# A third bank for the exponents' scores, and the first feed-forward units as steps of the last attention group

## What is computed

```python
x = _layernorm(x + attn0(x))   # 16 heads of 16, causal, softmax(q k / 4) v, then w_out and b_out
x = _layernorm(x + ffn0(x))    # hidden 1024; wu, wg, wd are ternary: silu(x wu) * (x wg), then wd
x = _layernorm(x + attn1(x))   # 16 heads, 4 key/value heads; ALiBi bias; pairs inside a window of
                               # +-32 or with i < 64 or j < 64 are masked out; q from x * sigmoid(sum|x|)
x = _layernorm(x + ffn1(x))    # silu(x w_gate) * (x w_up), then w_down
```

## Time and profile before

| | us |
|---|---|
| median of 3 runs | 1046.7 |
| the profiled execution | 1047.7 |
| its span, first to last instruction | 1046.0 |
| TensorE, VectorE, ScalarE, GpSimd busy | 978.5, 696.0, 598.1, 348.4 |
| mean granted TensorE clock | 0.975 |
| layer 0: first exponent | 86.2 |
| layer 0: last group, and the barrier behind it | 299.6 to 338.3 |
| layer 1: first exponent | 511.3 |
| layer 1: last group, and the barrier behind it | 844.4 to 895.4 |

### The profile page before, as it was taken

The page is one execution under the profiler, slowest core; times in us unless marked ns, Lnnn a source line. Parts: engine busy times, 40 slices in busy tenths (PEclk is TensorE's granted clock), DMA queues, the critical chain, the costliest instruction groups (busy, mean ns, idle before and its releaser), DMA issues. The chain is left out here.

```text
span 1046.0 us, 18023 instructions
## 1 busy us (share of the span) xinstructions
PE 978.5 (94%) x6546; PEld 515.4 (49%) x6546; DVE 696.0 (67%) x1535; ACT 598.1 (57%) x1204; POOL 348.4 (33%) x418
## 2 busy tenths in 40 slices
PE   6798999999988999987899999999999999899997
PEld 4452333333334888663334343333434344698896
DVE  2877878888835666578887878788788824325423
ACT  4344777777775435344476777777676767322321
POOL 3031222221212445232336363433425243224323
PEclk9797999999999999999899999999999999999999
DMA  7552111212000200151615050322301000000001
GB/s 252 173 172 97 57 31 38 63 61 62 2 2 3 89 1 1 39 170 57 182 38 171 1 171 8 123 73 59 105 28 38 1 2 1 1 1 21 21 1 41
DMA packets 32996, 64.20 MB, mean 61 GB/s; under 512 B 6095, under 2 KB 22367, under 8 KB 30532
## 3 DMA queue, kind: packets, MB, share of 16 engines
q1 hardware_dynamic: 31564, 58.47, 18.1%
q0 software_dynamic: 1072, 3.80, 1.1%
q10 hardware_dynamic: 272, 0.79, 0.2%
HBM read 50.45 MB, written 12.32 MB: 60 GB/s over the span
## 5 line engine op out<-in xcount | busy, mean ns | idle before, releaser
L1102 ACT ACTIVATE prob<-ps 128x512 f32<-128x512 f32 (+6 forms) x896 | 434.6, 536 | 183.8 <-PE ps L1145 176.2
L1145 PE MATMUL ps<-qop,kop 98*128 98x512 bf16 (+14 forms) x1376 | 279.5, 290 | 4.7 <-ACT prob L1102 1.2
L1131 PE MATMUL ps<-kop,qop 96*128 96x512 bf16 (+3 forms) x896 | 232.3, 361 | 18.7 <-DVE maxes L1037 14.6
L1145 PEld LDWEIGHTS ps<-qop,kop 107*128 107x128 bf16 (+1 forms) x1376 | 105.6, 98 | 253.4 <-ACT prob L1102 211.0
L1174 PE MATMUL ps<-prob,vst 128*32 128x512 f32 (+4 forms) x1792 | 212.3, 545 | 6.2 <-POOL prob L974 3.3
L1037 DVE CUSTOM_DVE_ANT_0 sums<-ps,tri 128x128 bf16<-128x128 f32 (+7 forms) x256 | 181.5, 754 | 32.1 <-PE ps L1131 27.6
L974 POOL TENSOR_TENSOR prob<-prob,keep 128x384 int32<-128x384 int32 (+2 forms) x144 | 122.8, 854 | 205.6 <-ACT prob L1102 204.4
L1037 DVE CUSTOM_DVE_ANT_0 sums<-ps,table 128x960 bf16<-128x960 f32 x128 | 148.1, 1157 | 58.2 <-PE ps L1131 44.4
L1570 PE MATMUL ps<-xs,wffn 128*128 128x512 f32 x640 | 156.2, 398 | 3.7 <-PEq L805 2.2
L1037 DVE CUSTOM_DVE_ANT_0 tri<-ps,table 128x960 bf16<-128x960 f32 x128 | 147.6, 1153 | 4.3 <-PE ps L1131 4.3
L1468 POOL TENSOR_TENSOR hs<-hf,hs 128x512 fp32r<-128x512 f32 x64 | 83.0, 1298 | 158.1 <-ACT hs L1495 158.0
(11 more groups left out here) (103 smaller groups left out, 685.8 us busy)
## 6 DMA issues: line engine op xcount, KB each, us to landing
table<-in_table SPq DMA_DIRECT2D x32, 464.0 KB, 4.7
qop<-q_parts SPq DMA_DIRECT2D x96, 128.0 KB, 2.6
kop<-k_parts SPq DMA_DIRECT2D x48, 128.0 KB, 2.6
kop<-k_parts SPq DMA_DIRECT2D x48, 96.0 KB
q_parts<-qop SPq DMA_DIRECT2D x8, 384.0 KB, 3.8
q_parts<-kop SPq DMA_DIRECT2D x8, 384.0 KB, 2.6
x<-in_x SPq DMA_DIRECT2D x4, 512.0 KB, 5.8
k_parts<-qop SPq DMA_DIRECT2D x4, 384.0 KB, 2.7
```

The lines of the kernel that those rows point to most:

```text
L1102: nc.scalar.activation(prob[0:rows, q % 2, k % HG, lo % CH:lo % CH + hi - lo], ps[0:rows, t_bank(n, k), lo % CH:lo % CH + hi - lo], ACT.Ex ...
L1131: last = nc.tensor.matmul(ps[:, S_BANK + score_slot(L, k)[0] + a // CH, a % CH:a % CH + b - a], qop[0:RD, par, h, i0:i0 + P], kop[0:RD, pa ...
L1145: return nc.tensor.matmul(ps[:, bank, a % CH:a % CH + b - a], lhs, rhs, start=start, stop=True, skip_group_check=True)
```

## The change

Five things. (1) Exponents, rows and norms take the banks 7, 4 and 5 in turn, in the order in which the plan has them, up to `FREE`; from there the exponents have their four banks as before and rows and norms bank 7. A table (`home`, `tenant`) is laid out ahead; each waits for the tenant before it in its bank. (2) The places of the maxima are new: new tables in layer 0, in layer 1 one behind the first exponent of a quad and one behind the third, where both were behind the second. `VALUES_BEHIND` puts the values behind the fourth exponent in most quads. (3) The opening of layer 1 has 3 maxima of group 1, not 4. (4) In layer 0 each step of the preparation stands two quads earlier, and the places of chunk 2's steps inside the feed-forward stages move one or two units later. (5) Unit 0 stands behind the last-but-one step of values, unit 1 behind the last norm, both ahead of the barrier, with their work on ScalarE and VectorE (unit 0's product; unit 1's comes behind the barrier).

```diff
-AHEAD = (6, 4)
+AHEAD = (6, 3)
...
-GIVEN = ("1101 1210 0200 0110 0220 1101 2020 2001 1010 2110 0200 0102",
-         "0210 1100 0210 0200 1102 0010 2110 0011 0100 3110 0200 1002")
-
-VALUES_BEHIND = ((4, 4, 4, 2, 3, 2, 3, 2, 4, 4, 3), (3, 4, 3, 3, 2, 4, 2, 3, 4, 4, 3))
+GIVEN = ("1012 0021 1010 1001 1121 0101 2021 2000 1000 3011 1100 1011",
+         "0210 1010 1200 0200 1100 2002 1200 1100 1000 2021 1100 1002")
+
+VALUES_BEHIND = ((4, 4, 3, 3, 4, 4, 4, 4, 4, 4, 4), (3, 4, 3, 4, 3, 4, 4, 4, 4, 4, 4))
...
         if layer.index == 1 and late:
-            return done if h == 0 else due
+            return (done + (due - done + 1) // 2, done, due, due)[h]
         return done + -(-(due - done) // (HG - h))
...
     if last:
-        steps += [(what, k, 0) for what, k in tail]
+        steps += [(what, k, 0) for what, k in (("ffn", 0), *tail, ("ffn", 1))]
         steps = with_preparation(steps, nq)
...
         if step[0] == "values" and step[2] == 0:
-            out += [(what, c, 0) for what, c in at.get(step[1], ())]
+            out += [(what, c, 0) for what, c in at.get(step[1] + (2 if nq == 12 else 0), ())]
...
-    T_BANKS, LAST_T_BANKS = (4, 5), (4, 5, 2, 3)
+    RING_BANKS, LAST_T_BANKS = (SIDE, 4, 5), (4, 5, 2, 3)
...
+        home, tenant = {}, {}
+
+        def lay_out():
+
+            last, turn, free = {}, 0, False
+            for group in range(-1, N):
+                for what, k, later in plan(L, group) if group >= 0 else opening:
+                    n = group + later
+                    if what not in ("exp", "rows", "norm"):
+                        continue
+                    free = free or (what == "exp" and n * NX + k >= FREE)
+                    if free:
+                        bank = LAST_T_BANKS[k % 4] if what == "exp" else SIDE
+                    else:
+                        bank, turn = RING_BANKS[turn % 3], turn + 1
+                    home[what, n, k], tenant[what, n, k] = bank, last.get(bank)
+                    last[bank] = (what, n, k)
+
+        def wait_given_back(pe, what, n, k):
+
+            if tenant[what, n, k] is None:
+                return
+            before, m, j = tenant[what, n, k]
+            if before == "exp":
+                pe.wait_ge(exp_done, m * NX + j + 1)
+            elif before == "rows":
+                pe.wait_ge(m_copied, m + 1)
+            else:
+                pe.wait_ge(normed, 2 * m + j + 1)
...
+                    elif what == "ffn":
+                        if k == 0:
+                            pe.wait_ge(proj.tern if i == 0 else w_cut, (9, 12)[i])
+
+                            pe.wait_ge(prep.n_lo, 2 * KD)
+                        else:
+
+                            pe.wait_ge(exp_done, N * NX)
+                        after.unit(pe, k)
...
-    BETWEEN = {0: [("gather", 2)], 1: [("turn_attn", 2), ("copy_attn", 2)], 4: [("project", 4), ("project", 5), ("add", 2)],
-               5: [("inverse", 2), ("gather", 3)], 7: [("normalise", 2)], 9: [("turn_x", 2), ("high", 2), ("low", 2)],
+    BETWEEN = {2: [("gather", 2)], 3: [("turn_attn", 2), ("copy_attn", 2)], 5: [("project", 4), ("project", 5), ("add", 2)],
+               6: [("inverse", 2), ("gather", 3)], 8: [("normalise", 2)], 10: [("turn_x", 2), ("high", 2), ("low", 2)],
...
     def pe(self, pe):
-        self.unit(pe, 0)
-        self.unit(pe, 1)
         for c in range(NC):
```

More of the change, by code:

```diff
@@ L756, in load_keys, with attend @@
                             else k.unsqueeze(1).to_broadcast((HD, L.key_sets, T))).then_inc(landed, 16)
-def attend(nc, sem, K, L, dram, prep, before):
+def attend(nc, sem, K, L, dram, prep, before, after):
     i = L.index
@@ L813, in attend @@
         opening = opening_of(L, proj)
[L815 to L826, removed]
+        home, tenant = {}, {}
[23 more added lines that the diff above has]
+                pe.wait_ge(normed, 2 * m + j + 1)
+        lay_out()
         def all_groups(step):
@@ L1111, in step @@
                         nc.scalar.copy(ot[:], ps[:, O_BANK, :]).then_inc(evicted, 1)
+                    elif what == "ffn":
+                        after.act_unit(act, k)
                     elif what in Projection.STEPS:
@@ L1202, in step @@
                             proj.wait_read(pe, *proj.last_on[SIDE])
[L1203 to L1206 removed]
+                        wait_given_back(pe, "rows", n, 0)
+                        nc.tensor.transpose(ps[:, home["rows", n, 0], :].bitcast(BF16)[:, 0:P],
                                             mpart[:].rearrange("p k u -> p (k u)"), identb[:]).then_inc(m_turned, 1)
@@ L1483, in pool_tail, with round_hidden, act_unit @@
             self.prep.inverse(pool, chunk(NC - 1, k), 1)
-    def act(self, act):
-        nc, K = self.nc, self.K
-        hf, sg, ps = K.hf, K.sg, K.ps
-        def round_hidden(u):
-            c, e = u // KE, u % KE
-            act.wait_ge(self.hid, u + 1)
-            if c >= 1 and e == 0:
-                act.wait_ge(self.down_full, 2 * c)
-            nc.scalar.copy(self.hidden(e, 0), hf[:, u % 2, :]).then_inc(self.h_hi, 1)
-        for u in range(NC * KE):
-            act.wait_ge(self.up_full, u + 1)
-            if u >= 2:
-                act.wait_ge(self.hid, u - 1)
-            nc.scalar.activation(sg[:, u % 2, :], ps[:, 2 * (u % 2), :], ACT.Silu,
-                                 scale=K.scales[:, 0:1] if self.i == 0 else 1.0).then_inc(self.silu_done, 1)
-            if u >= 1:
-                round_hidden(u - 1)
+    def round_hidden(self, act, u):
+        c, e = u // KE, u % KE
+        act.wait_ge(self.hid, u + 1)
+        if c >= 1 and e == 0:
+            act.wait_ge(self.down_full, 2 * c)
+        self.nc.scalar.copy(self.hidden(e, 0), self.K.hf[:, u % 2, :]).then_inc(self.h_hi, 1)
+    def act_unit(self, act, u):
+        K = self.K
+        act.wait_ge(self.up_full, u + 1)
+        if u >= 2:
+            act.wait_ge(self.hid, u - 1)
+        self.nc.scalar.activation(K.sg[:, u % 2, :], K.ps[:, 2 * (u % 2), :], ACT.Silu,
+                                  scale=K.scales[:, 0:1] if self.i == 0 else 1.0).then_inc(self.silu_done, 1)
+        if u >= 1:
+            self.round_hidden(act, u - 1)
+    def act(self, act):
+        for u in range(2, NC * KE):
+            self.act_unit(act, u)
             for what, k in self.between(u):
@@ L1696, in build @@
             K.operands = Operands(nc, sem, K, L, dram)
-            attend(nc, sem, K, L, dram, prep, before)
-            before = FeedForward(nc, sem, K, L, dram, prep)
+            after = FeedForward(nc, sem, K, L, dram, prep)
+            attend(nc, sem, K, L, dram, prep, before, after)
+            before = after
         alone(nc, before)
```

49 lines of the change are left out of this document (24 added, 25 removed).

## The result

Median 1010.4 us (1007.9 to 1011.0, 4 runs) against 1046.7 (1045.0 to 1048.1, 4 runs): ratio 0.965 (95%: 0.963 to 0.967), 3.5% faster, inside the forecast's own 1009 to 1023, 6 us below its point of 1016.5. The profiled execution took 1011.0 us, its span is 1009.3 us (before 1046.0). TensorE's mean granted clock rose from 0.975 to 0.983.

What follows compares the result with a forecast made beforehand. Matmul-bound TensorE was taken to hide about 0.10 us of bank wait a quad; 9.6 + 11.8 + 2.6 + 5.0 + 1.2 = 30.2 us off the profiled 1047.7 gives 1017.5, median forecast 1016.5 us (1009 to 1023; wider range 1006 to 1033).

Steps and rivals of the forecast that it cites:

- TensorE is full: Rival: the third bank does nothing and only the two ends give, 1040.5 us; chance 0.05.
- Waits change hands: Rival: TensorE then waits for VectorE's maxima or masks; half the groups' 24.0 us stays, 1028.5 us; chance 0.19.
- More than I take: Rival: all of the floor's rest goes and both ends give well, 1002 to 1008 us; chance 0.09.
- Of 2.0 us I take 1.6: Layer 1's groups: of 2.0 us above the 45.3 us floor, 1.6 goes; six full groups give 9.6 us.
- 1.7 of 2.3: Layer 0's groups: of 2.3 us above the 27.7 us floor, 1.7 goes; groups 1 to 5 give 8.5 us.
- the spacing of maxima: Layer 1's quads: maxima 0.8 and 1.8 us apart, each finished before its slot is wanted; nothing waits, quad 2.58 us.
- group 0 of layer 0: Layer 0's first group, 34.5 us at a clock of 0.86: gain of 2.0 us.
- the last group of layer 0: Layer 0's end with two units: early waits -1.6, x wait net -0.9, boundary -0.7, clock -1.8; sum -5.0 us.
- the opening of layer 1: Layer 1's start: one early maximum fewer gains 0.6 us, group 0's own bank waits 2.0; together 2.6 us.
- The slower rivals: Norms or rows hold the ring, 1062 us, chance 0.05; or the clock falls to 0.86, 1090 us, chance 0.02.
- break-even of 0.72 us a hold: Ring-held rival: 42 holds in fourteen groups; at 0.72 us each the loss decides against the 30 us gained.
- once a group (the other norm has the values behind it): A norm's hold of a ring bank makes the third exponent behind it start some 0.3 us late, once a group.

Runs made afterwards that it cites:

- the ring alone: Kernel before with only the third bank (exponents, rows and norms on 7, 4, 5); order, opening, preparation and units as before: 1026.9 us, ratio 0.981.
- the change again: The changed kernel run once more, unaltered, in a later job as yardstick: 1011.6 us (1009.4 to 1012.5).
- pairs in layer 1: Changed kernel with layer 1's maxima both behind the second exponent again, layer 0's new tables kept: 1008.6 us, ratio 0.964.
- four early maxima: Changed kernel with 4 maxima of group 1 in layer 1's opening again, not 3: 1009.0 us (1006.8 to 1012.8).
- ring and order: Kernel before with third bank and new places of maxima and values; opening, preparation and first units as before: 1019.0 us, ratio 0.974.
- the new order alone: Kernel before with only the new places of maxima and values, still two exponent banks: 1072.5 us, ratio 1.025.
- units and no shift: Changed kernel with layer 0's preparation two quads later again, the first units still ahead of the barrier: 1016.7 us (1014.1 to 1018.5).

## Why the prediction came out as it did

**Right: what bounds the kernel.** That a busy column of 47.1 of 47.3 us hid 0.1 us of bank wait a quad, read from start to start, was the step on which the forecast stood. The quad came out at 2.57 us (2.58 forecast; its terms add up to 2.59), groups at 45.3 and 28.0 us, against floors of 45.3 and 27.7. "TensorE is full" fell with the ring alone. "Waits change hands" fell too: a middle group of either layer has no row with a waiting matmul (TensorE is busy 27.9 of 28.0 and 45.3 of 45.3 us). In the groups the rival "More than I take" was right; the ends didn't give what it wanted.

**Too small: "Of 2.0 us I take 1.6", "1.7 of 2.3".** I kept a fifth to a quarter of the floor's rest back for VectorE. Layer 1 gave 1.9 a group and layer 0 2.1. VectorE held nothing up in the middle groups but for a norm's hold, 0.13 to 0.14 us a group. That is 3.8 us of the 6.5 by which the sum was short.

**Wrong in its reason: the spacing of maxima.** I took layer 1's gain from the new order. The ring alone reaches it with the old one. The new order matters in layer 0 only, 1.3 us a group; which of its two tables does it, that of the maxima or that of the values, wasn't tried apart.

**Too small: group 0 of layer 0**, 4.1 for 2.0. The half level of the clock reached 9.8 us into the group before and 3.0 after (0.86 and 0.95 in the windows); at half rate these 6.8 us are worth at most 3.4. What the group gave beyond the 2.1 of its neighbours, 2.0, lies within that. Traces with the same code in this group show the price: with the half level to 3.0 us into it the group takes 30.3 us, to 4.8 us (the change again) 30.8, to 6.2 us (pairs in layer 1) 31.4. So 0.3 to 0.5 us go with each, and 2.0 for the 6.8 fits that. But where the half level ends differs between two executions of the one kernel, so this part isn't all the change's doing: in the second trace the group gave 3.6. The 1.7 us ahead of the first exponent are of the same kind, 13.6 us of half level before (without the stretch that reaches into the group), 6.8 after, 10.2 when the change ran again, and they helped the sum by luck. I had put the clock in one place only, layer 0's end.

**Too large: the last group of layer 0**, 3.9 for 5.0. The early waits fell from 2.0 to 0.8 us, -1.2 where I took -1.6. The wait that was to follow the 2.44 ("1.0 to 1.5 us") came as 1.52 for x and 0.56 for a mask, 2.1 in all: "net -0.9" was -0.4. The boundary gave 0.5 for 0.7 (0.62 us are left, under 0.5 was forecast). The clock held and gave its 1.8, but not as summed: I took 0.223 us a matmul for a unit, alone it takes 2.05 us, 0.256 a matmul, so that two cost 4.1 us and not 3.6; in return the last values and the norm's transposes, 0.63 and 1.12 us at the half level before, took 0.43 and 0.66. The eviction's 0.70 stayed, as forecast, but not because ScalarE's copy queues behind the unit's Silu: ScalarE idles 0.62 us in front of the copy, and the wait is the copy itself, 0.58 us directly behind the values.

**Half right: the opening of layer 1.** 2.3 for 2.6, but not for the reason given. The opening gave nothing: from the end of layer 0's two units to layer 1's first exponent are 167.6 us, 167.7 before. All 2.3 are group 0's (48.2 us for 50.5), and with four early maxima the time is the same or lower.

**The slower rivals.** The ring is held, and the price of a hold is real: lengthened, norms cost 10.5 us. The break-even of 0.72 us a hold was far off; the dearest ones in the change cost 0.13 to 0.14, where I had allowed 0.3. My step "once a group (the other norm has the values behind it)" holds in layer 1, not in layer 0: there both norms are at the limit. The clock didn't fall: 1.00 in the middle groups of every variant, with two banks in the cycle and with three. By the failure that the Trainium skill's page "TensorE: Matmul & The Clock Gate" (A second HAM failure mode) describes it might have; here TensorE idled less, not more.

**The change's last parts.** From ring and order to the whole change are 8.6 us by medians, 7.6 by spans; 3.3 of these stand in layer 0's end and 2.6 behind the start of layer 1's last group. Of the 2.6 the change of code explains 1.0; the other 1.6 is a half level of 3.4 us (from 865.1) that ring and order has there and the change has not. The kernel before has the same waits at that place without it, so it can't be put down to the units. Most of the rest, 1.4, stands ahead of the first exponent, where the code is the same.

**Slips of the sums.** The lower end (0.6 us in each of the 14 groups with maxima, tails of 1.5) is a gain of 9.9 us and not 11; nothing hung on it.

## What to carry to other kernels

Measure a TensorE-bound loop from start to start, add up its steps at the pace each has where nothing holds it, and compare with the period: what is missing is a wait, whatever the busy column says; then see in the rows of the weight loads who is waited for. When a ring of buffers grows, change the order of work with it and try each alone: two banks want pairs of exponents with other work between, three take either order in layer 1 and want the new one in layer 0, and the new order alone cost 26 us. Before a short tenant joins a ring, see how long its reader takes, and lengthen it once: that tells which of its holds have slack. Where a sum is tested by a single trace, take a second one: here 1.7 us of the gain were in a stretch that the change doesn't touch, and the repeat didn't have 1.4 of them.

## What the runs showed that I had not expected

- Ring and order were worth 34 us more together than their single effects added up.
- A values step of 4 x 32 columns behind an exponent's scores costs 0.06 to 0.09 us in front, with two banks (0.085 with the order alone), with three (0.09) and with four (0.06 to 0.07). It is no wait for a bank.
- The half level of the clock appears in stretches of 3.4, 6.8, 10.2 or 13.7 us, and they differ between executions of one kernel: without the one at the program's very end, 47.7 us before, 30.6 after, 34.0 when the change ran again. Ahead of layer 0's first exponent the same code has 10.7 us of it in one trace and 15.7 in the other. Single executions of one kernel lie up to 4.4 us from their median, 0.4%; how much of that is the clock's isn't shown.
- With units and no shift, TensorE idles 2.44 and then 1.66 us, and the half level begins inside the second wait (318.4) and lasts 10.2 us. The change idles 1.52 and 0.56 us there and keeps its clock.
